# Constants of a two-layer kernel gathered in one 128-byte tensor, which moves TensorE's operands of the last stage to multiples of 128 bytes

## The reference: what is computed

```python
x = x + layernorm(attn(layernorm(x)))     # attn: rmsnorm, 256->768 projection, 3-tap causal convolution,
                                          # a 4096-tap convolution from 16 poles per channel, gating,
                                          # out projection, then y + W3(gelu(W1 y') * (W2 y')), 672 hidden
x = x + layernorm(ffn(layernorm(x)))      # ffn: 256->1024, exact gelu, 1024->256; both weights get
                                          # a rank-one correction from rows 1..16 of the batch
```

## Time and profile before

| | |
|---|---|
| median of 3 runs | 1077.09 us (1076.13 to 1077.38) |
| profiled execution, first to last instruction | 1076.4 us |
| stages A and B (0 to 247.1 us of the span) | 247.1 us |
| stage C (247.1 to 1071.5 us) | 824.4 us |
| TensorE busy over the span | 1052.2 us, 98% |
| VectorE, ScalarE, GpSimd busy | 82%, 66%, 28% |
| granted TensorE clock over the span | 1.000 |

### The profile page before, as it was taken

The page is one execution under the profiler, slowest core; times in us unless marked ns, Lnnn a source line. Parts: engine busy times, 40 slices in busy tenths (PEclk is TensorE's granted clock), DMA queues, the critical chain, the costliest instruction groups (busy, mean ns, idle before and its releaser), DMA issues.

```text
span 1076.4 us, 24951 instructions
## 1 busy us (share of the span) xinstructions
PE 1052.2 (98%) x9012; PEld 1009.4 (94%) x9012; DVE 881.6 (82%) x2322; ACT 710.0 (66%) x1589; POOL 300.1 (28%) x575
## 2 busy tenths in 40 slices
PE   8899999999999999999999999989999999999998
PEld 7777888899989999999999999989999999999997
DVE  7999998874788878888887888898878888887776
ACT  6879887864456666666666665656666666666644
POOL 7677775460101111111111111111112111111111
PEclk9999999999999999999999999999999999999999
DMA  4337988987432333333333333543333333333000
GB/s 129 119 116 235 292 219 194 375 309 144 88 66 42 54 57 50 51 52 54 57 67 57 53 51 60 132 86 41 60 50 50 51 53 54 59 63 60 21 21 31
DMA packets 112491, 102.83 MB, mean 96 GB/s; under 512 B 7552, under 2 KB 103744, under 8 KB 112112
## 3 DMA queue, kind: packets, MB, share of 16 engines
q1 hardware_dynamic: 111136, 98.67, 41.9%
q0 software_dynamic: 736, 2.51, 0.7%
q10 hardware_dynamic: 496, 0.05, 0.0%
HBM read 75.75 MB, written 30.70 MB: 99 GB/s over the span
## 4 chain that ended last, share of the span: by engine, by line
PE 67%; DVE 6%; issue 2%; ACT 1%; POOL 0%; DMA 0%; SPq 0%; POOLq 0%; DVEq 0%; ACTq 0%
PE ps_ring L1546 35%; PE ps_w L1546 16%; PE ps_m L1546 9%; PE ps_o L1546 4%; PE ps_rt L1561 2%; DVE base L1368 1%; PE ps_w L1556 1%; DVE bn L1272 1%; PE ps_m L1612 1%; DVE prod L1315 0%; DVE ht_l L1284 0%; DMA base<-in_w 0%; DVE pt_l L1284 0%; POOL sc L1124 0%; DVE yrow L1507 0%
## 5 line engine op out<-in xcount | busy, mean ns | idle before, releaser
L1124 POOL TENSOR_TENSOR sc<-sc,neg_half 128x2 f32<-128x2 f32 x127 | 94.8, 746 | 677.8 <-DVE sc L1496 405.7
L1189 ACT ACTIVATE gate<-ps_ring 128x256 f32<-128x256 f32 x192 | 73.0, 381 | 127.4 <-PE ps_ring L1546 126.4
L1210 ACT ACTIVATE hid<-ps_ring,b1s 128x256 f32<-128x256 f32 x256 | 112.4, 484 | 27.7 <-PE ps_w L1546 13.5
L1546 PE MATMUL ps_ring<-mt_l,wl_h 128*128 128x256 f32 x640 | 125.8, 278 | 2.6 <-DVE mt_l L1284 2.6
L1546 PE MATMUL ps_ring<-mt_h,wl_h 128*128 128x256 f32 x640 | 125.7, 278 | 1.9 <-DVE prod L1315 1.3
L1546 PE MATMUL ps_ring<-mt_h,wl_l 128*128 128x256 f32 x640 | 125.2, 277 | 0.0
L1284 DVE TENSOR_TENSOR ht_l<-hid,ht_h 128x256 fp32r<-128x256 f32 x256 | 103.2, 423 | 16.8 <-ACT ht_h L1214 10.9
L1546 PE MATMUL ps_ring<-xt_h,we_h 128*128 128x256 f32 x512 | 103.5, 283 | 2.8 <-DVE prod L1315 2.4
L1315 DVE TENSOR_TENSOR prod<-ps_ring,gate 128x256 f32<-128x256 f32 x192 | 80.7, 421 | 24.6 <-ACT gate L1189 20.8
L1546 PE MATMUL ps_ring<-xt_h,we_l 128*128 128x256 f32 x512 | 100.2, 277 | 0.0
L1546 PE MATMUL ps_ring<-xt_l,we_h 128*128 128x256 f32 x512 | 100.2, 277 | 0.0
(11 more groups left out here) (203 smaller groups left out, 2732.8 us busy)
## 6 DMA issues: line engine op xcount, KB each, us to landing
toep_scratch<-taps_scratch SPq DMA_DIRECT2D x26, 512.0 KB, 7.5
toep<-toep_scratch SPq DMA_DIRECT2D x26, 512.0 KB, 8.5
xa<-in_x SPq DMA_DIRECT2D x16, 512.0 KB, 5.0
x_scratch<-x2c SPq DMA_DIRECT2D x16, 512.0 KB, 3.7
x2s<-x_scratch SPq DMA_DIRECT2D x32, 256.0 KB, 6.9
xa_c<-in_x SPq DMA_DIRECT2D x32, 256.0 KB, 2.7
xb_c<-in_x SPq DMA_DIRECT2D x32, 256.0 KB, 2.7
yin<-seq SPq DMA_DIRECT2D x124, 64.0 KB, 6.1
```

What stands on the lines that cost most here:

```text
L1124: nc.gpsimd.tensor_tensor(sc[:, to], sc[:, to], neg_half[:, 0, 0:CC], ALU.pow).then_inc(S[done], 1)
L1189: nc.scalar.activation(gate[rows_of, m % 2], ring[m % RING][rows_of, 0], ACT.Gelu_apprx_tanh).then_inc(S["gate_done"], 1)
L1210: nc.scalar.activation(hid[:, m % HIDS], block_of, ACT.Gelu, bias=b1s[:, m:m + 1]).then_inc(S["hid_done"], 1)
L1546: mm = nc.tensor.matmul(out, lhs(a, kk), rhs(b, kk), start=(j == 0), stop=(closed and j == len(todo) - 1))
```

## The change

`neg_half`, `neg_one`, `mark`, `b1s`, `scale_s` and `to_end` are no longer tensors of their own but columns of one tensor `small` of 32 float32 columns (128 bytes) right behind `ident`. Nothing else is edited. The sum of what lies ahead of a tensor is then a multiple of 128 up to `bn`: `norm_scale`, `norm_shift`, `x2s`, `yin`, `seq`, all weights and all activations of stage C named above start at remainder 0. What stage A and B allocate behind `ahead` (`win`, `zn`, `zt`, `toep`, `spread`, `state`) stays where it was. The tiny tensors from `bn` on (`mva`, `sc`, `shift`, `sums`) move by 32 bytes.

```diff
+SMALL = 32
...
         ident = sb(whole, "ident", [P, P])
-        neg_half = sb(whole, "neg_half", [P, 2, CA])
-        neg_one = sb(whole, "neg_one", [P, CC])
+        small = sb(whole, "small", [P, SMALL])
+        neg_half = small[:, 0:2 * CA].rearrange("p (a c) -> p a c", a=2)
+        neg_one = small[:, 2 * CA:2 * CA + CC]
+        mark = small[:, 2 * CA + CC:2 * CA + CC + 1]
+        b1s = small[:, 16:16 + HB]
+        scale_s = small[:, 16 + HB:17 + HB]
...
-        mark = sb(whole, "mark", [P, 1])
...
-            to_end = sb(early, "to_end", [P, 1])
+            to_end = small[:, 17 + HB:18 + HB]
...
+    b1s, scale_s = v["b1s"], v["scale_s"]
...
-        b1s = sb(ctx, "b1s", [P, HB])
         b2s = sb(ctx, "b2s", [P, D])
-        scale_s = sb(ctx, "scale_s", [P, 1])
```

## The result

The changed kernel takes 1105.77 us in the median (1104.94 to 1106.25, 4 runs) against 1077.07: a ratio of 1.0256, 95% interval 1.0224 to 1.0287. It is slower by 28.7 us, on the side of the first rival and not of the forecast. (The profiled execution took 1106.25 us with a span of 1104.5, so what lies around the span is some 1.7 us in one execution, and not the 0.7 that was read before the prediction; a difference of spans can still be read as one of times.)

What follows compares the result with a forecast made beforehand. TensorE's matmul chain in stage C was taken to bound the kernel; only the alignment term counted: 1077.1 - 27 = 1050 us. The 8-in-10 range was 1033 to 1110; faster 0.50, same 0.17, slower 0.33.

Steps and rivals of the forecast that it cites:

- the first rival: Stage C: operands at equal remainders by 128 disturb each other; 1098 us at 118 ns, 1110 at 120; chance 0.27.
- What bounds the kernel, and that only the pace matters: Stage C, 824.4 of 1076.4 us, is a matmul chain of count times pace; other engines' timing hardly matters.
- the reading of the 272 cycles: Stage C's 256-column matmuls: misaligned pieces touch 17 blocks of 64 bytes instead of 16, at 16 cycles each, giving 272.
- the term of -27 us: Stage C: alignment saves 4.4 ns on each of 6110 matmuls, 27 us in all.
- term (6): Stage C: moving and stationary operands of the 256-column matmuls go to remainder 0, the one part expected to gain.
- The signs named beforehand: In the changed trace: 48 up products 5.23 us instead of 5.45, step 23.6, idle wout_h matmuls from 120 to some 115.
- two rivals: Stage A's 233 ns fits operands disturbing each other (0.27), or 17 cycles per 16 columns wherever placed, so no change (0.17).
- Stage A as a witness: Stage A's aligned 512-column matmuls take 233.1 ns, where full pace by alignment would be about 218; evidence against the forecast.
- The third rival's mixture: Stage C: 44 of 206 matmuls run at 118 ns; all moving to 113.3 gains 8 us (1069); chance 0.08.
- The parts costed at nothing: Tensors made columns, stages A and B, DMA addresses, VectorE and ScalarE operands in stage C: each put at 0 or unseen.

Runs made afterwards that it cites:

- The blocks at distance 0: Changed kernel with idle matmuls of wl1_h added at its end, 40 per block, both operands at one address: 120.0 ns with 128 stationary columns, 113.3 with 32.
- the block at 128: Changed kernel with 40 idle matmuls of 128 by 512 columns from wl1_h added at its end, operands 128 bytes apart: 232 ns each.
- the run with 64 bytes: Changed kernel with 64 unused bytes ahead of the activations of stage C: 1076.93 us, ratio 0.9995 to the kernel before.
- the run with 192: Changed kernel with 192 unused bytes ahead of the activations of stage C: 1078.62 us, ratio 1.0016 to the kernel before.

## Why the prediction was wrong

**What bounds the kernel, and that only the pace matters**, held: stage C grew by 28 us, stages A and B by a no more telling 0.2, and no other engine's busy time changed by more than 2.5 us in stage C. TensorE's idle time there fell from 7.9 to 6.6 us.

**The step that failed is the reading of the 272 cycles**, "If a block costs 16 cycles, 17 cost exactly the 272 measured". The number fitted, but so did other rules, 17 cycles for 16 columns among them. Three runs speak against the block: with both operands on multiples of 64, 64 bytes apart, the pace is still 113.3; with both moved off by 32 at distance 0, it is still 120 and not more; and 512 columns take 544 cycles where 32 blocks would take 512. So the gain of 4.4 ns per matmul, the term of -27 us, was not there at all: no piece or block of 256-column matmuls ran below 113.3 in any run, to rounding. What the change did was to bring the two operands of every pair to the same place, which term (6) of the sum had at no cost: 120.0 instead of 114.6 ns, 5.4 ns lost per matmul and 28.7 us in all. The signs named beforehand came out the other way: the 48 up products took 5.76 us and not 5.23, and the idle matmuls stayed at 120. The 262 cycles that the prediction quotes from the Trainium skill ("TensorE: Matmul & The Clock Gate", section Back-to-back issue gap) were not reached either; 272 is the least measured here for 256 columns of this type, and 544, against the 518 there, for 512. I had written that it was an inference from one number, and two rivals explained the row of stage A that spoke against it.

**The first rival was right** that operands in the same place disturb each other, and nearly in size, with the 120 ns of the earlier trace rows; it had the period at 128 bytes, and it is 256. It gave 1110 us and 1105.8 was measured. A step lost 1.08 us, as 206 x 5.4 ns = 1.11 says, but not every step could. At the start of each of the two batches there is a stretch in which VectorE's work sets the pace. These are the rows of the chain at which it goes back to TensorE (start us, us, work), in the kernel before and then in the changed one:

```profile
327.62 2.38 PE ps_ring L1546 x18
...
730.57 2.38 PE ps_ring L1546 x18
```

```profile
328.24 2.39 PE ps_ring L1549 x18
...
745.04 2.39 PE ps_ring L1549 x18
```

Up to the first row, 80 us into stage C, only 0.6 us is lost: from 272 us on the chain there runs mostly over VectorE (`base`, `bn`, `mt_l`, `pt_l` and others), and slower matmuls hide behind it. From the first row to the second 13.9 us are lost, another such stretch included, and 13.6 us in the rest. The prediction said that such waits were not in its sum. Even the first unit's up products, at 7.91 us already slow before, take 8.00 now. The prediction sets beside this rival the rule of the Trainium skill ("TensorE: Matmul & The Clock Gate", section Step-by-step: what each phase is for) that loading the next weights takes no read bandwidth from the running matmul. The blocks at distance 0 don't agree with it: 120.0 ns with loads of 128 columns, 113.3 with loads of 32.

**Stage A as a witness** was half right. Its 233 ns goes with the distance (128 modulo 256, like the block at 128 with 232, and 227.5 once it was a multiple of 256), but not with equal remainders modulo 128, which was how I put the rival. With 512 moving columns distance 0 is the good place, with 256 moving columns the bad one. A place found for one shape doesn't carry over to another.

**The third rival's mixture** is real: two paces of one distance, 113.3 and 118. Distance modulo 256 doesn't tell which: the run with 64 bytes has the distances of the kernel before and its slow share in other products, in each step alike. It has about the time of the kernel before, as has the run with 192. A distance that keeps all of stage C at 113.3, worth some 8 us, was not found (144, whose block ran at 113.5, was not tried in the whole kernel); what starts or ends the pace of 118 stays open. So does whether it is the load of the next matmul that disturbs, or its own: both have the same address modulo 256 within a product, and no run parts them.

**The parts costed at nothing** (the memsets and loads into one tensor, VectorE's and ScalarE's operands, the DMAs, stage B) cost nothing that can be told. The run with 64 bytes has all of the change in it, with `small`, `x2s`, `yin`, `seq` and the weights at their new places, and takes the time of the kernel before (ratio 0.9995, 0.9984 to 1.0006).

## What to carry to other kernels

Where `float32r` matmuls of 128 stationary by 256 moving columns run back to back, look at the distance between the two operands' addresses modulo 256 bytes and not at the alignment of each: bringing all of them to distance 0 was the slowest of the six distances tried in the whole kernel, together with 256, and cost 2.6%. 64 unused bytes gave it back. Other types were not run, and with 512 moving columns distance 0 was the fastest, so measure the shape at hand. Matmuls of a tensor with itself in the trace show the pace of distance 0 before anything is changed. And when one number fits a mechanism exactly, write down which other mechanism it fits as exactly, and look for a row or a run in which they differ; here a second length of the stream would have done.

## What the hardware showed that was not expected

- The least that a stream of `float32r` took at 2.4 GHz was 113.3 ns (272 cycles) for 256 columns and 227 (544) for 512, also with weight loads of 32 columns and wherever it started (remainders 0, 32 and 64 by 128); 384 columns took 174 ns at two distances.
- With 128 stationary and 256 moving columns the pace was 6.2 to 6.7 ns over that least at distances of 0, 256, 512 and 768 bytes, and 9.5 over it at 4 bytes (122.8). At 144 it was at the least in the one block run.
- One distance has more than one stable pace. Of six blocks at 192 modulo 256, three ran at 113.5 to 114.0 ns and three at 117.8 to 118.0; of three at 16, one at 113.3, one at 116.8 and one at 118.8, and one at 272 at 118.8.
- With 512 moving columns the order of the distances is another: 227 at 0 and 256, 229 at 64, 232 at 128 and 16, 233 at 192. With 64 stationary columns at 0 it was 230.
